# A perceiver kernel on one core: the context's first piece cut to one batch, the first local keys set ahead of the queries' projection, the first weights issued by ScalarE, the order written anew

## What is computed

```
x = x + L0_xattn(layernorm(x), ctx)          # local attention: query i sees its own 16 of 512 keys
x = x + L0_rwkv(layernorm(x))                # running-maximum recurrence over 32 tokens
x = x + L0_moe(layernorm(x))                 # 8 experts, 2 taken, and a shared one
x = x + L1_xattn(layernorm(x), ctx, mask)    # full attention, 16 heads of 8
x = x + L1_linear_attention_and_ffn(layernorm(x))
x = x + L1_moe(layernorm(x))                 # 16 experts, capacity 32, one taken
```

## Time and profile before

| | us |
|---|---|
| runs | 235.16, 236.79, 237.21 |
| median | 236.79 |
| the profiled execution | 235.32 |
| its span (first to last instruction) | 233.4 |
| TensorE busy in it | 218.7 |
| VectorE, ScalarE, GpSimd busy | 178.0, 131.7, 34.5 |

### The profile page before, as it was taken

How to read it: one execution, slowest core, us unless ns; L and a number is a source line. 1 busy time by engine, 2 the same in 40 slices (tenths; PEclk the granted TensorE clock), 3 DMA queues, 4 the chain that set the end, 5 groups by cost and what they waited for, 6 DMA issues and landing times.

```text
span 233.4 us, 5227 instructions
## 1 busy us (share of the span) xinstructions
PE 218.7 (94%) x1992; PEld 156.2 (67%) x1992; DVE 178.0 (76%) x514; ACT 131.7 (56%) x292; POOL 34.5 (15%) x55
## 2 busy tenths in 40 slices
PE   7699999999999999879989998999999989898995
PEld 6332595747786796546656776768577768797495
DVE  2176743999955669999788979999998958646672
ACT  2201473445368327689999987988887741030330
POOL 2120000022205123602040230020001031201000
PEclk9999999999999889999999999999999999999999
DMA  6999959700000000006100340000005998500001
GB/s 204 412 421 448 420 219 213 150 0 0 1 3 0 0 3 0 1 3 159 24 0 0 95 91 3 3 0 4 0 3 177 449 442 386 219 0 0 3 3 45
DMA packets 2905, 26.88 MB, mean 115 GB/s; under 512 B 448, under 2 KB 704, under 8 KB 1344
## 3 DMA queue, kind: packets, MB, share of 16 engines
q1 hardware_dynamic: 2880, 26.54, 31.3%
HBM read 26.28 MB, written 0.26 MB: 114 GB/s over the span
## 4 chain that ended last, share of the span: by engine, by line
PE 72%; DVE 15%; ACT 6%; issue 3%; DMA 3%; SPq 0%; POOL 0%; DVEq 0%
PE bank L1452 8%; PE bank L1328 6%; PE bank L1306 6%; PE bank L1438 6%; PE bank L1266 5%; PE bank L1469 4%; DVE ctx_sb L964 4%; PE bank L1270 3%; DMA ctx_sb<-ctx 3%; PE bank L1411 2%; PE bank L1694 2%; ACT ctx_sb L583 2%; PE bank L1249 2%; PE bank L1394 2%; PE bank L1584 2%
## 5 line engine op out<-in xcount | busy, mean ns | idle before, releaser
L583 ACT ACTIVATE ctx_sb<-ctx_sb,small_sb 128x512 f32<-128x512 f32 x64 | 45.8, 720 | 3.1 <-DVE small_sb L964 3.1
L964 DVE CUSTOM_DVE_ANT_0 ctx_sb<-bank,mask_sb 128x512 f32<-128x512 f32 x64 | 42.2, 683 | 1.7 <-PE bank L1438 1.5
L1452 PE MATMUL bank<-early_sb,ctx_sb 128*128 128x128 f32 x256 | 36.3, 278 | 3.1 <-DVE work_sb L975 2.7
L1452 PEld LDWEIGHTS bank<-early_sb,ctx_sb 128*128 128x128 f32 x256 | 27.9, 141 | 14.6 <-issue 7.9
L385 POOL TENSOR_TENSOR rstd_sb<-veps_sb,minus_half_sb 128x2 f32<-128x2 f32 (+1 forms) x15 | 11.0, 733 | 128.8 <-DVE veps_sb L684 128.8
L594 ACT COPY work_sb<-bank 128x512 f32<-128x512 f32 x40 | 22.9, 579 | 7.7 <-PE bank L1452 7.0
L1438 PE MATMUL bank<-k_sb,work_sb 32*128 32x512 f32 x128 | 18.5, 638 | 1.7 <-DVE small_sb L964 1.1
L1266 PE MATMUL bank<-ctx_sb,early_sb 128*128 128x512 f32 x32 | 16.3, 610 | 1.8 <-DMA ctx_sb<-ctx 1.8
L732 DVE SCALAR_TENSOR_TENSOR work_sb<-bank,early_sb,work_sb 128x512 f32<-128x512 f32 x16 | 11.8, 747 | 8.2 <-PE bank L1306 7.7
L1469 PE MATMUL bank<-work_sb,v_sb 128*32 128x128 f32 x512 | 17.3, 276 | 0.4 <-ACT work_sb L594 0.4
L1270 PEld LDWEIGHTS bank<-late_sb,ctx_sb 128*128 128x128 f32 x128 | 15.4, 191 | 2.8 <-issue 2.6
(11 more groups left out here) (262 smaller groups left out, 403.4 us busy)
## 6 DMA issues: line engine op xcount, KB each, us to landing
k_sb<-moe_w SPq DMA_DIRECT2D x1, 4096.0 KB, 12.8
ctx_sb<-moe_w SPq DMA_DIRECT2D x1, 4096.0 KB, 17.2
ctx_sb<-ctx SPq DMA_DIRECT2D x3, 1024.0 KB, 15.4
late_sb<-late SPq DMA_DIRECT2D x1, 2966.5 KB, 21.7
mask_sb<-ctx_tok SPq DMA_DIRECT2D x1, 2048.0 KB, 14.3
v_sb<-ctx_tok SPq DMA_DIRECT2D x1, 2048.0 KB, 27.8
mask_sb<-mask SPq DMA_DIRECT2D x4, 512.0 KB, 7.9
mask_sb<-mask SPq DMA_DIRECT2D x8, 256.0 KB, 4.5
```

The lines of the kernel that those rows point to most:

```text
L583: s.activation(sc[u % NSC], sc[u % NSC], ACT.Exp, bias=smin[:, u:u + 1], scale=-1.0, accum_out=rsum[:, u:u + 1]).then_inc(sig("p1_ready"), 1)
L964: v.tensor_tensor_reduce(sc[u % NSC], bank[SB[u % GROUPS]][:, :], mask[:, KEYS * b:KEYS * (b + 1)], MASK_BIG, 3e38, ALU.add, ALU.min, smin ...
L1452: last = nc.tensor.transpose(bank[TB[u % 2]][:, P * k:P * (k + 1)], sc[u % NSC][:, P * k:P * (k + 1)], wt("ident"))
```

## The change

ScalarE's block begins with the issue of early, which SyncE no longer has. The context's first piece is batch 0 alone, its second batch 1 alone; so there are six pieces, of 1, 1, 2, 4, 4 and 4 batches, and SyncE issues the first four right behind x. TensorE's wait for early is moved ahead of the first `yield`. The local key matrix of batch 0 becomes a step of its own between the turning and the queries' projection; layer 1's projection of batch 1, which stood there, now stands behind the queries' projection. All four strings are new.

```diff
 TURNS = {
     "PE": (
-        "L P L P L11 P4 L P L8 P L2 a L2 P L a P L a3 P L P L4 P6 a P L P2 L3 a L2 a2 L P L P L a L a P a2 b "
+        "L P L3 P L9 P4 L P L8 P L2 a L P L2 a P L a3 L P L2 P L2 P6 L P a L P L3 a L a2 L2 P L a L a L P L "
...
     "DVE": (
-        "L23 a L a L a L a4 L a L2 a4 L a5 L a L2 a4 L a L a2 L a L2 P a2 L a2 b L3 a L2 P L a5 L P a4 b a6 P "
+        "L23 a2 L2 a L a4 L a L2 a4 L a2 L a3 L a L a2 L a L a3 L3 a2 P L2 a4 L4 a P L a4 b a2 L a4 b a P a4 "
...
     "ACT": (
-        "L2 P3 L P2 L a L5 P L2 P2 L a P2 a3 P a P a2 P3 L P3 L2 P L a L a L a3 L2 a L a3 P L b P b2 a P b a "
+        "L P L P2 L P2 L3 a L3 P L2 P2 L P a P a3 P a3 P3 L P4 L3 a L2 P a2 L a3 L2 a2 L2 a P b P b2 a P b4 P "
...
-        PIECES = (0, 2, 4, 8, 12, BATCH)
+        PIECES = (0, 1, 2, 4, 8, 12, BATCH)
...
             sp.dma_start(x_tok[:, :], x_d).then_inc(sig("x_in"), 16)
-            sp.dma_start(early[:, :], early_d).then_inc(sig("early_in"), 16)
             context(0)
             context(1)
             context(2)
+            context(3)
             sp.dma_start(following[:, :], next_d).then_inc(sig("next_in"), 16)
             sp.dma_start(ctok[0], ctok_d[:, 0:CTX // 2]).then_inc(sig("ctok_in0"), 16)
-            context(3)
+            context(4)
             sp.dma_start(late[:, :], late_d).then_inc(sig("late_in"), 16)
-            context(4)
+            context(5)
...
             s = nc.scalar
             turned = [0, 0]
+            s.dma_start(early[:, :], early_d).then_inc(sig("early_in"), 16)
...
-                yield
                 pe.wait_ge(sig("early_in"), 16)
+                yield
                 turn_lnT(0, X[0], range(TT))
+                yield
+
+                def keys(c):
+
+                    mm(bank[c % 2][:, :], wt("wk0"), ctx[:, KEYS * c:KEYS * (c + 1)], start=True, stop=True).then_inc(sig("k0_ps"), 1)
+
+                pe.wait_ge(sig("ctx_in0"), 16)
+                keys(0)
                 yield
                 wait_norm(0)
                 mm(Y[0][:, :], wt("wq0"), lnT[:, :], start=True, stop=True).then_inc(sig("q0_ps"), 1)
...
                     for c in range(HB * h, HB * (h + 1)):
-                        if c in PIECES:
...
+                        if c:
...
+                            keys(c)
+                            yield
```

More of the change, by code:

```diff
@@ L69 @@
     "PE": (
[6 rows of a table removed]
-    "DVE": (
[7 rows of a table removed]
-    "ACT": (
[4 rows of a table removed]
[6 rows of a table added]
+    "DVE": (
[7 rows of a table added]
+    "ACT": (
[5 rows of a table added]
     "POOL": (
-        "L a L a4 b a3 b L a3 b2 a b4 a b a b3 L c3 d c d L a c d2 a c L b2 d c L c b2 d3 a c b d2 c ")}
+        "L2 a6 b a2 b a4 b10 c L2 c2 b a2 d c d c d b d b L d c d a d L b a c d b d c2 a d L a d c L b c ")}
 class Shifted:
@@ L1277, in local @@
                     mm(bank[2][:, 0:256], q1T[:, 0:P], q1T[:, 0:256], start=True, stop=True)
+                pe.wait_ge(sig("early_in"), 16)
                 yield
-                pe.wait_ge(sig("early_in"), 16)
                 turn_lnT(0, X[0], range(TT))
+                yield
[3 more added lines that the diff above has]
+                keys(0)
                 yield
@@ L1299, in local @@
                     for c in range(HB * h, HB * (h + 1)):
-                        if c in PIECES:
[L1301 to L1306, removed]
-                        yield
+                        if c:
+                            if c in PIECES:
+                                pe.wait_ge(sig(f"ctx_in{piece_of(c)}"), 16)
+                            if c % HB >= 2:
+                                pe.wait_ge(sig("prod_ready"), c - 1)
+                            elif h:
+                                pe.wait_ge(sig("z_out"), HB)
+                            keys(c)
+                            yield
                         if c % 4 == 3 and c % HB > 4:
```

## The result

| | before | after |
|---|---|---|
| median of 19 runs each, same chip | 235.16 | 235.57 |
| lowest, highest | 232.34, 237.80 | 234.25, 237.69 |
| the profiled execution | 235.32 | 237.13 |
| its span | 233.4 | 235.3 |

A forecast was written before the change was run, and what follows sets the result against it. TensorE, busy in 218.7 of 233.4 us, was taken as the bound. The start's 1.45 us, all else 0, gave 233.87 from the profiled 235.32, or 235.3 against the median of 236.79; range 232.6 to 237.8.

The forecast's parts named there:

- Gain in front of the queries' projection 1.45.: At the start, before the queries' projection: 1.88 us sooner less 0.43 lost by x, bounds 1.0 and 1.9.
- its first long piece is a transfer, the first piece of the context: Start of the chain: a context transfer issued at 1.64, awaited 6.57 us, landing at 8.21, ahead of TensorE's first projection.
- rival 1: At the start the late context still decides: only 0.3 to 1.0 us gained, time 236.2 at 0.6; chance 0.14.
- x loses 0.43.: At the start x, sharing the DMA engines with early, lands 0.43 us later, bounds 0 and 0.86.
- When the blanks end, 6.44.: At the start TensorE's 14 blank matmuls end at 6.44 us, when it can take the first projection.
- The keys ahead cost 0: Between turning and queries: the first local key matrix replaces batch 1's projection and covers ScalarE's copy, cost 0.
- SyncE 0: SyncE's queue of loads: one issue goes and one comes, later loads issued as before; cost 0, at most 0.1 us.
- ScalarE's copy hidden: At the start ScalarE copies batch 0's projection from about 7.3 to 8.0, before the turned tiles at 8.06; no cost.
- The order behind: After the start: some 1100 steps permuted on four engines, none added; taken as 0, with -1.1 and +1.1 us kept.
- Rival 3: Within the scores, VectorE's expert choice of half 1 comes later and takes the gain back: 237.7 to 239.3; chance 0.16.
- Rival 3's sign of recognition: The lead is there at 80 us and gone by 135, with TensorE waiting for VectorE's or GpSimd's queries.
- Rival 2: Half-clock stretch around 82 us vanishes (1.6 us) or the new order saves 1.1: 234.0, both 232.6; chance 0.20.

The follow-up runs named there:

- E1: The kernel before run once more, unchanged; ratio 1.0022 (0.9973 to 1.0071).
- E2: The new start with the old order of steps behind it, against the kernel before: ratio 0.9971 (0.9919 to 1.0024), median 234.38.
- G3: The kernel before with early issued by ScalarE and TensorE's wait for it a step ahead: ratio 1.0016 (0.9974 to 1.0058).
- E4: The changed kernel with early issued by SyncE right behind x: ratio to before 1.0115 (1.0030 to 1.0199, 6 runs).
- F4: E2 with early issued by SyncE behind x, so old order: ratio to before 0.9940 (0.9890 to 0.9990), median 234.02.
- F3: The changed kernel with six more unread matmul steps (G) in TensorE's string: ratio to before 1.0061 (1.0025 to 1.0097), median 234.66.
- E3: The kernel before's start with the new order behind it: ratio to before 1.0106 (1.0069 to 1.0144), median 236.00.
- G4: F4 with one TensorE projection moved between two matmul pairs and VectorE's copy two steps later: ratio to before 1.0093 (1.0054 to 1.0133).
- F1: New start and new order up to the first scores step, then the old order: ratio to before 1.0049 (1.0005 to 1.0093).

## Why the prediction was wrong

**"Gain in front of the queries' projection 1.45."** Measured between the two first profiles 1.13 at the queries (10.68 to 9.55), 1.28 at the fifth key matrix. The size is within its bounds, but its base was not the usual one. The first step that failed is: "its first long piece is a transfer, the first piece of the context". That was true of the one execution read. In E1 the same program had the context 1.8 us sooner (6.43 against 8.21) and was held by its own blanks, and the new start is then worth 0.1 (E2 against E1). I had the row that could have warned me: the context's 6.57 us against early's 3.0 in the same queue, which I noted under rival 1 and used only against the new kernel's start.

**"x loses 0.43."** It lost 1.0: it starts VectorE at 4.50 against 3.54, and 4.56 against 3.54 in G3. Over the upper bound of 0.86, which assumed that all of early goes ahead of x's last bytes; early took 0.9 longer as well. In the eight profiles with ScalarE's issue x landed at 4.25 to 4.92, in the six with SyncE's at 3.35 to 3.61. The rule of the Trainium skill that I weighed (DMA: Bandwidth & Descriptors, "Issuing engines are not separate DMA queues") says that transfers issued by several engines interleave on the same 16 DMA engines and only the issue is saved; the traces agree, with 3.7 us for x beside early and 2.7 ahead of it. The one that paid was x, for which the chain waits. Undone, the change of issuer gives 0.97 where the blanks are short (E4); where they run to 7.2 or later, x is hidden either way (G3).

**"When the blanks end, 6.44."** I took this for a constant. The same 14 matmuls took 5.13, 5.93, 4.70, 5.75, 4.89, 5.99, 4.94 and 6.18 us in eight profiles. Over all 14 profiles the range is the same, 1.5 us, and it moves the start by more than either edit. After's 4.70 was the shortest of all, which was luck.

**"The keys ahead cost 0", "SyncE 0", "ScalarE's copy hidden".** In after nothing waited for any of them: L500 ran 7.00 to 7.69, ahead of the turned tiles at 8.69. In F4, where the tiles come a us sooner, it is no longer hidden: there the chain runs through that copy (7.38 to 8.06) and then L488. The condition I gave, context and tiles far enough apart, was met only because x was late.

**The order behind, "I take 0 and keep -1.1 and +1.1".** This is the second step that failed, and it decided the result. The order costs 1.8 us in A at like clock, some 2.0 in the runs at clock 1.00 (F3 against F4), 0.7 to 1.1% by E3. Half of it is lost by steps ordered before the scores, where the prediction looked at nothing. The rest comes in small pieces through the scores. That "none is added" was true, but eight steps of G were taken out, and I had not counted them. Rival 3's chain is late there as I counted (20 score steps for 17, 24 for 22) and closes up as I said (3.4 us shrinks to 1.3 by the copy), and its net price is small, 0.14 us by the table: so rival 3 as one mechanism with one place fell too, though its sum, more than the start gives, is what happened. The bound "a third of TensorE's 3.35 idle us, either way" was taken from idle time; a worse order makes new idle time, and has no such limit. Rival 3's sign of recognition even came true, the lead there at 80 us and gone by 135, but 1.6 of those 2.6 us are the fall at 127.

**The clock.** Rival 2 held that the fall at 82 us might go and give 1.6. It went and gave that (the lead was 0.8 at 65 us, when the order had taken 0.5 of the 1.28, and 2.6 at 89), and I had written "nothing in the edit works on the clock". The order does: in every profile with the old strings unchanged the fall lies at 78 to 80 if there is one in A, with the new ones at 124 to 127 (G4, with one step moved, has it at 126.7), and with the new ones in the tail at 196 to 201; and of the runs with the whole new order and its idle tail (after, E3, E4) none of 37 was at clock 1.00, of before 10 of 29. So the gain was given back at 127 and once more at 199, where after also idled for VectorE. F3 shows the second as caused at least in part by that idle time. Why a fall comes at 127 no run shows: TensorE was busy for all of the 3.1 us before it and idle for 0.48 in the 4 us before those.

**Together.** By E2's ratio the start brings -0.7 us (not told from 0), by E3's the order costs +2.5; the sum, +1.8, is near the 1.6 of the ratio. By the medians over all runs it is 0 and +1.6, which do not add up to the +0.4 of the change: only the order's sign is sure, by the runs alone. In the profiles 1.8 of the order's cost is seen at like clock in A; how the rest splits isn't shown. The range held the median (235.57 in 232.6 to 237.8), the sign was wrong.

## What to carry to other kernels

Before taking a gain from the start of a trace, ask which of its waits repeat: two profiles of the same kernel here differed by 1.3 us in 15. An order written by hand over several engines is one object, whose cost is neither bounded by the idle time that it finds nor the sum of the waits that it makes; price it by marks on the bounding engine, at like clock, and by a run with the new order alone. A load that is wanted later should not be put on a second queue beside the load that the chain waits for.

## What was not expected of the hardware

- The granted clock fell to 1.2 GHz for 3.4 or 6.8 us at a time, and each 3.4 us cost 1.4 to 1.6 us in A. The mean granted clock groups the runs of one kernel (230.8 us at 1.00, 232.4 at 0.993, 234.6 at 0.978), a wider spread than most edits here make.
- 14 equal blank matmuls at the start took 4.70 to 6.18 us. The first follow each other at 0.43 us, the last at 0.215, and where the pace doubles differs: after 4.03 us in after, 4.88 in before, 6.59 in E1, and in F1 and G4 not before the last blank. Until then their starts agree to 0.01 us in all 14 profiles. The granted clock reads 1.00 on both sides of it. 5 to 6 us, in before and then in E1 (columns as above):

```profile
5.00:6.00 1.00, 1.00 (x6) 0.90 (x5) 0.03 (x1) 0.00 (x0) 0.82 (x1) 1.00 0.80 262
```

```profile
5.00:6.00 1.00, 1.00 (x4) 0.82 (x3) 0.00 (x0) 0.00 (x0) 0.99 (x2) 1.00 1.04 324
```

- Two transfers of 256 and 294 KB issued within 0.01 us by two engines landed after 3.7 and 3.9 us; issued by one engine 0.4 us apart they took 2.7 and 3.0 each.
- 512 KB of context, third in the queue, took 6.57 us in one execution and 4.79 in another of the same program.
